# Graph attention kernel, first stage: transposing raw rows, normalisation moved behind the product with W, table written in half groups

## What is computed

```python
def _L0_gnn_ref(h, adj, W, a):
    Wh = h @ W
    a1, a2 = (a[:Fout, 0], a[Fout:, 0])
    e = (Wh @ a1)[:, None] + (Wh @ a2)[None, :]
    e = jnp.where(e > 0, e, ALPHA * e)
    e = jnp.where(adj > 0, e, MASK_VAL)
    attention = jax.nn.softmax(e, axis=1)
    return jax.nn.elu(attention @ Wh)

x = x + _L0_gnn_ref(_layernorm(x, axis=-1), adj, L0_gnn_W, L0_gnn_a)
x = x + _L0_ffn_ref((_layernorm(x, axis=-1))[None], ...)[0]
```

## Time and profile before

| | |
|---|---|
| median of three runs | 1185.75 us |
| profiled execution, span from first to last instruction | 1177.2 us |
| median less span (what lies around the instructions, and the spread between runs) | 8.55 us |
| first stage, up to the last table row (0 to 143.7 us) | 12% of the span |
| wait for the table to land | 143.7 to 160.2 us |
| second stage | about 160 to 1020 us |
| busy: PE, VectorE, ScalarE, GpSimd | 884.0, 891.8, 796.2, 655.2 us |
| DMA traffic | 357.33 MB, mean 304 GB/s |

### The profile page before, as it was taken

How to read it: one execution, slowest core, us unless ns; L and a number is a source line. 1 busy time by engine, 2 the same in 40 slices (tenths; PEclk the granted TensorE clock), 3 DMA queues, 4 the chain that set the end, 5 groups by cost and what they waited for, 6 DMA issues and landing times.

```text
span 1177.2 us, 24953 instructions
## 1 busy us (share of the span) xinstructions
PE 884.0 (75%) x4321; PEld 558.7 (47%) x4389; DVE 891.8 (76%) x4327; ACT 796.2 (68%) x1339; POOL 655.2 (56%) x700
## 2 busy tenths in 40 slices
PE   2777728788888878888788878876878765568995
PEld 1545514454444444544444444543544444346674
DVE  5788637888888888888788888876887876555563
ACT  1544639788878888888678887866887821146663
POOL 3555445565556556655566656654655656236664
PEclk9999959999999999999899999988998986679998
DMA  7678679999999999999899999988998995035551
GB/s 258 249 277 316 250 278 370 359 379 382 366 375 377 366 372 378 380 359 379 328 354 377 381 375 374 384 314 306 383 373 316 329 249 130 25 112 162 174 167 59
DMA packets 84715, 357.33 MB, mean 304 GB/s; under 512 B 26006, under 2 KB 52591, under 8 KB 68289
## 3 DMA queue, kind: packets, MB, share of 16 engines
q1 hardware_dynamic: 56226, 296.78, 67.9%
q0 software_dynamic: 27712, 60.06, 14.9%
q10 hardware_dynamic: 736, 0.05, 0.0%
HBM read 343.67 MB, written 32.05 MB: 319 GB/s over the span
## 4 chain that ended last, share of the span: by engine, by line
DVE 27%; DMA 22%; issue 21%; PE 9%; POOL 6%; DVEq 2%; POOLq 0%; ACT 0%; ACTq 0%
DMA regions<-x,posu 13%; DMA G_all<-wh_table,idx 7%; POOL G_all L617 4%; DVE top_word L900 2%; PE psO L1718 2%; DMA out_x<-raw_all,tok 2%; DVE xn L1170 2%; PE psO L1591 2%; POOL out_x L679 1%; DVE begun L1070 1%; DVE lidx L1185 1%; DVE oh L1193 1%; DMA wh_table<-mean_sb 1%; DVE el L1144 1%; DVE lmax L1180 1%
## 5 line engine op out<-in xcount | busy, mean ns | idle before, releaser
L617 POOL DMA_INDIRECT G_all<-wh_table,idx x384 | 397.7, 1036 | 137.8 <-issue 131.0
L725 ACT ACTIVATE sg<-raw_all,minus_tiny 128x1024 fp8e4<-128x1024 int32 x256 | 311.5, 1217 | 0.1
L728 ACT ACTIVATE sg<-raw_all,minus_half 128x1024 fp8e4<-128x1024 int32 x256 | 311.4, 1216 | 0.0
L1516 PE MATMUL psO<-word_no,share 128*128 128x512 bf16 x827 | 220.5, 397 | 3.7 <-issue 0.9
L639 POOL DMA_INDIRECT regions<-x,posu x64 | 67.4, 1053 | 209.2 <-DVE idx L1062 111.8
L1591 PE MATMUL psO<-G_all,diag 128*128 128x256 f32 x640 | 162.9, 404 | 22.3 <-DVE diag L1127 22.3
L1591 PEld LDWEIGHTS psO<-G_all,diag 128*128 128x128 f32 x640 | 123.6, 201 | 64.5 <-issue 48.3
L1525 PE MATMUL psF<-sg,fold_w 128*128 128x512 bf16 x512 | 136.5, 390 | 7.5 <-DVE top_word L900 2.7
L1516 PEld LDWEIGHTS psO<-word_no,share 128*128 128x128 bf16 x885 | 90.7, 107 | 86.4 <-issue 15.4
L758 ACT ACTIVATE pr<-ee,nmx 128x16 f32<-128x16 f32 x64 | 19.7, 308 | 153.9 <-DVE nmx L1118 153.9
L900 DVE MAX8 top_word<-psF 128x8 f32<-128x256 f32 x256 | 103.0, 425 | 15.4 <-remote 9.6
(11 more groups left out here) (227 smaller groups left out, 1901.7 us busy)
## 6 DMA issues: line engine op xcount, KB each, us to landing
raw_all<-in_adj SPq DMA_DIRECT2D x128, 2048.0 KB
raw_all<-regions SPq DMA_DIRECT2D x84, 130.0 KB, 2.1
wh_table<-G_all POOLq DMA_DIRECT2D x8, 1040.0 KB, 11.8
x_sb<-in_x SPq DMA_DIRECT2D x8, 1024.0 KB, 5.8
G_all<-wh_table,idx POOLq DMA_INDIRECT x384
regions<-pad_row SPq DMA_DIRECT2D x32, 130.0 KB
x_sb<-in_L_ffn_W SPq DMA_DIRECT2D x4, 512.0 KB
x_sb<-in_L_ffn_W SPq DMA_DIRECT2D x8, 256.0 KB
```

The source lines that it names most:

```text
L617: pool.indirect_dma_start(out=G[par][:, k, :], out_offset=None, in_=table[:, :], in_offset=bass.IndirectOffsetOnAxis(ap=idx[par][:, k:k + ...
L725: act.activation(sign_of[par][q][0], raw_of[b][q % 2][0], ACT.Identity, bias=minus_tiny[:, 0:1], scale=TINY, saturate=False)
L728: act.activation(sign_of[par][q][1], raw_of[b][q % 2][1], ACT.Sign, bias=minus_half[:, 0:1], saturate=False).then_inc(a_sg, 1)
L1516: pe.matmul(psO[par][:, :], share[:, :], word_no[:, 0:2, :].rearrange("p q w -> p (q w)"), start=True, stop=True)
```

## The change

- TensorE transposes the raw rows of `x_sb`; `normalise`, its four `xn` buffers and the semaphore `v_xn` are gone. The first product is then x·W' with W' = W_aug - (1/256)·(ones·W_aug), which equals (x - mean)·W_aug.
- W' is made once: TensorE multiplies a matrix of ones with `w_aug` (new line 1476), VectorE subtracts the result over 256 (new line 1025, two instructions on 128 x 258).
- The division by the deviation moves into the eviction: VectorE `table_rows` (new line 975) multiplies PSUM by `rs` where it copied. It stands first in each strip and has no lag; `COPY_LAG` is gone.
- Table rows go out in half groups (`CHUNK` = 4, 520 KB), right behind the fourth and the eighth strip, 16 issues for 8. `row_sum` adds up table rows (258 columns) for the first 60 strips; the last four are added by TensorE at the end, straight from `table_rows_sb`, so the mean row needs one product less.
- `load_group` waits only until the load before the last has landed (none for the first two).
- Set-up: TensorE waits for W and a alone and for five constants; the router matrix and bias have semaphores of their own. The clearing of `G_all` is cut to its two padding columns. `fold_w`, `word_no`, `rw_t`, `hT` and `count` move behind the statistics of group 0. Two small writes of a padding row into the table are gone.

```diff
-            sp.dma_start(w_raw[:, :, :], gW.rearrange("(h p) n -> p h n", p=P)).then_inc(const_in, 16)
+            sp.dma_start(w_raw[:, :, :], gW.rearrange("(h p) n -> p h n", p=P)).then_inc(w_in, 16)
 
             def load_group(g, par, i):
 
-                sp.wait_ge(v_xn, g * GROUP + 2)
-                sp.nop(nofuse=True)
+                if i:
+                    sp.wait_ge(xg_in[par], i * 16)
+                    sp.nop(nofuse=True)
                 sp.dma_start(x_sb[:, bass.ds(g * GROUP, GROUP), :],
                              x[bass.ds(g * GROUP * P, GROUP * P), :].rearrange("(r p) d -> p r d", p=P)
...
-            def row_sum(s, r):
-
-                pool.wait_ge(v_xn, s + 1 + 2 * GROUP)
+            def row_sum(g, par, r):
+
+                s = g * GROUP + r
+                pool.wait_ge(v_wh, s + 1 + 2)
                 if s:
                     pool.wait_ge(pl_sum, s)
                 pool.nop(nofuse=True)
-                pool.tensor_tensor(xn_sum[:, :], xn_sum[:, :], xn[r % 4][:, :], ALU.add).then_inc(pl_sum, 1)
-
-            def write_rows(g, par):
-
-                pool.wait_ge(v_wh, g * GROUP + GROUP + 2)
+                pool.tensor_tensor(row_total[:, :], row_total[:, :], table_rows_sb[par][:, r, 0:D + 2], ALU.add).then_inc(pl_sum, 1)
+
+            def write_rows(g, par, r):
+
+                pool.wait_ge(v_wh, g * GROUP + r + CHUNK + 2)
                 pool.nop(nofuse=True)
-                pool.dma_start(table[bass.ds(g * GROUP * P, GROUP * P), :].rearrange("(r p) d -> p r d", p=P),
-                               table_rows_sb[par][:, :, :]).then_inc(tab_out[par], 16)
+                pool.dma_start(table[bass.ds((g * GROUP + r) * P, CHUNK * P), :].rearrange("(r p) d -> p r d", p=P),
+                               table_rows_sb[par][:, r:r + CHUNK, :]).then_inc(tab_out[par], 16)
 
             def group(g, par, i, behind, ahead):
                 for r in range(GROUP):
-                    row_sum(g * GROUP + r, r)
-                    if behind and r == COPY_LAG - 1:
-                        write_rows(g - 1, 1 - par)
+                    if g * GROUP + r < NS - CHUNK:
+                        row_sum(g, par, r)
+                    if r % CHUNK == CHUNK - 1:
+                        write_rows(g, par, r - CHUNK + 1)
                     if ahead and r == 5:
                         inverse_stds(g + 1)
             groups(pool, group)
...
-                act.dma_start(a_sb[:, :, 0:1], ga[D:2 * D, :].rearrange("(h p) o -> p h o", p=P)).then_inc(const_in, 16)
-                act.dma_start(a_sb[:, :, 1:2], ga[0:D, :].rearrange("(h p) o -> p h o", p=P)).then_inc(const_in, 16)
-            act.dma_start(rw_sb[:, :], rw[:, :]).then_inc(const_in, 16)
-            act.dma_start(rb_sb[:, :], rb.rearrange("(o n) -> o n", o=1).to_broadcast([P, E])).then_inc(const_in, 16)
+                act.dma_start(a_sb[:, :, 0:1], ga[D:2 * D, :].rearrange("(h p) o -> p h o", p=P)).then_inc(w_in, 16)
+                act.dma_start(a_sb[:, :, 1:2], ga[0:D, :].rearrange("(h p) o -> p h o", p=P)).then_inc(w_in, 16)
+            act.dma_start(rw_sb[:, :], rw[:, :]).then_inc(rw_in, 16)
+            act.dma_start(rb_sb[:, :], rb.rearrange("(o n) -> o n", o=1).to_broadcast([P, E])).then_inc(rb_in, 16)
...
-            v.memset(xn_sum[:, :], 0.0)
+            v.memset(row_total[:, :], 0.0)
+            v.memset(G_all[:, :, D + 2:ROW], 0.0)
...
-            v.memset(G_all[:, :, :], 0.0)
-            v.wait_ge(consts, 19)
...
-            def normalise(g, par, r):
+            def table_rows(g, par, i, r):
                 s = g * GROUP + r
 
+                v.wait_ge(pe_wh, s + 1 + 2)
                 if r == 0:
                     v.wait_ge(pl_rs, g + 1)
-                if s >= 4:
-                    v.wait_ge(pe_xT, s - 1)
-                    v.wait_ge(pl_sum, s - 3)
-                v.tensor_scalar(xn[s % 4][:, :], x_rows(s), mv[par][:, r, 0:1], rs[par][:, r:r + 1],
-                                ALU.subtract, ALU.mult).then_inc(v_xn, 1)
-
-            def table_rows(s):
-                g, r = divmod(s, GROUP)
-                i, par = divmod(g, 2)
-
-                v.wait_ge(pe_wh, s + 1 + 2)
-                if r == 0:
-                    v.wait_ge(tab_out[par], i * 16 + 16)
-                v.tensor_copy(table_rows_sb[par][:, r, 0:D + 2], psW[r % 2][:, 0:D + 2]).then_inc(v_wh, 1)
+                    if i:
+                        v.wait_ge(tab_out[par], i * 16 * GROUP // CHUNK)
+                        v.wait_ge(pl_sum, g * GROUP - GROUP)
+                v.tensor_scalar(table_rows_sb[par][:, r, 0:D + 2], psW[r % 2][:, 0:D + 2], rs[par][:, r:r + 1], None,
+                                ALU.mult).then_inc(v_wh, 1)
...
-                    normalise(g, par, r)
+                    table_rows(g, par, i, r)
...
-                    if g * GROUP + r >= COPY_LAG:
-                        table_rows(g * GROUP + r - COPY_LAG)
...
+            for h in range(DH):
+                v.wait_ge(pe_w, DH + 1)
+                v.tensor_copy(w_aug[:, h, D:D + 2], psL[:, 2 * h:2 * h + 2]).then_inc(v_w, 1)
+
+            for h in range(DH):
+                v.wait_ge(pe_w, DH + 2)
+                v.scalar_tensor_tensor(out=w_aug[:, h, :], in0=psW[1][:, 0:D + 2], scalar=-1.0 / D, in1=w_aug[:, h, :],
+                                       op0=ALU.mult, op1=ALU.add).then_inc(v_w, 1)
+            v.wait_ge(consts, 19)
...
+
+            v.wait_ge(pe_w, DH + 4)
+            v.tensor_scalar(mean_sb[:, 0:D + 1], psL[0:1, 0:D + 1], 1.0 / N, None, ALU.mult).then_inc(v_wh, 1)
...
-            pe.wait_ge(const_in, 16 * 5)
-            pe.wait_ge(consts, 19)
+            pe.wait_ge(w_in, 16 * 3)
+            pe.wait_ge(consts, 5)
...
+            pe.wait_ge(v_w, 3 * DH)
+            pe.nop(nofuse=True)
             for h in range(DH):
-                mm = pe.transpose(psW[0][:, h * E:(h + 1) * E], rw_sb[:, h * P:(h + 1) * P], ident[0:E, 0:E])
+                mm = pe.matmul(psW[1][:, 0:D + 2], ones_f[:, :], w_aug[:, h, :], start=(h == 0), stop=(h == DH - 1))
...
+            def transposes(s, g, par, i, r):
+
+                if r == 0:
+                    pe.wait_ge(xg_in[par], i * 16 + 16)
                 if s >= 3:
                     pe.wait_ge(a_xT, s)
                 pe.nop(nofuse=True)
                 for h in range(DH):
-                    mm = pe.transpose(psXn[s % 3][:, h * P:(h + 1) * P], xn[s % 4][:, h * P:(h + 1) * P], ident[:, :])
+                    mm = pe.transpose(psXn[s % 3][:, h * P:(h + 1) * P], x_sb[:, s, h * P:(h + 1) * P], ident[:, :])
                 mm.then_inc(pe_xT, 1)
 
...
                 for r in range(GROUP):
-                    transposes(g * GROUP + r, r)
+                    transposes(g * GROUP + r, g, par, i, r)
+                    if g * GROUP + r == 2:
+                        pe.wait_ge(v_w, 4 * DH)
                     if g * GROUP + r >= 2:
                         table_rows(g * GROUP + r - 2, r)
+                if g == 0:
+                    pe.wait_ge(v_fold_w, 2)
                 fold(i, i % 2, par)
...
-            pe.wait_ge(pl_sum, NS)
+            pe.wait_ge(pl_sum, NS - CHUNK)
+            pe.wait_ge(v_w, 4 * DH + 1)
             pe.nop(nofuse=True)
-            for h in range(DH):
...
+            pe.matmul(psL[0:1, 0:D + 2], ones_f[:, 0:1], row_total[:, :], start=True, stop=False)
+            for r in range(GROUP - CHUNK, GROUP):
+                pe.wait_ge(v_wh, NS - GROUP + r + 1 + 2)
+                pe.nop(nofuse=True)
+                mm = pe.matmul(psL[0:1, 0:D + 2], ones_f[:, 0:1], table_rows_sb[(NG - 1) % 2][:, r, 0:D + 2], start=False,
+                               stop=(r == GROUP - 1))
             mm.then_inc(pe_w, 1)
```

79 lines of the change are left out of this document (28 added, 51 removed).

## The result

The changed kernel takes 1154.57 us (median of 4 executions, 1146.12 to 1163.13) beside 1185.24 for the kernel before (4, 1184.41 to 1191.76): ratio 0.971, 95% interval 0.965 to 0.978, so 30.7 us faster. Forecast: 1152, range 1142 to 1168. The profiled execution took 1156.93 us with a span of 1155.2. Medians are of all executions; a ratio and its interval leave out executions more than 1.5% above the quickest of their kernel, so the two can differ by some tenths of a per cent.

What follows compares the result with a forecast made beforehand. The first stage was held bound by a ring of waits, the second near the DMA limit. A gather 35 us earlier, less 1 for emptier buffers, took the span from 1177.2 to 1143; plus 8.55 made 1152 us, range 1142 to 1168.

Steps and rivals of the forecast that it cites:

- Set-up: Start of the kernel: first eviction at about 18.8 us against 29.3, 10.5 us earlier, bounds 7 and 13.
- Group 0: First eight strips: four at 2.1 us, four at 1.1, a fold of 1.2; end at about 31 instead of 42.5.
- Odd groups: Groups 1, 3, 5 and 7 of the first stage: 10.3 us each, TensorE's pace in the last group.
- loads and clock: End of the first stage: 2 us added to 108, putting the last table row at 110 us.
- Even groups: Groups 2, 4 and 6, where VectorE also decodes: 12 us each, with no charge for table-write waits.
- the port rule: VectorE and GpSimd share a port pair locked per instruction; 0.6 us per group was to go with normalise.
- rival 1: First stage becomes DMA-bound: groups of 13 us, gather near 133, gain 27 or less, about 1160 us; chance 0.14.
- End of the stage: Last table row at 110 us, mean row issued 1.7 later and landing in 11, first gather at 125 instead of 160.2.
- Ring: First stage: waits among normalise, TensorE's transposes and products, and VectorE's evictions bind it, not DMA or a peak engine.
- GpSimd's power exposed in each group: First stage: GpSimd's chain binds in seven groups, costing 19 us of the 34, about 1170 us; chance 0.07.
- Writes one after another: First stage: half table writes land serially at 11.8 us each, 57 us later than 160, about 1240 us; chance 0.03.
- Second stage gives it back by the clock: Second stage: denser TensorE work lowers the granted clock earlier, costing 18 us, about 1170 us; chance 0.06.

Runs made afterwards that it cites:

- again: The changed kernel run once more, nothing altered, on the first chip: 1152.54 us, ratio 0.973 to the kernel before.
- again2: The changed kernel run once more, nothing altered, in the third group on a slower chip: 1241.33 us, ratio 0.976 to the kernel before.
- late37: The changed kernel with GpSimd additions that nothing needs ahead of the first gather: 1180.79 us, ratio 0.999 to the kernel before.
- setup_back: The changed kernel with the old set-up: all of G_all cleared, TensorE waiting for every small load: 1160.4 us, ratio 0.980 to the kernel before.
- gate: The changed kernel with each load of x held until the second eviction two groups earlier; slower chip: 1246.59 us, ratio 0.976 to the kernel before.
- dummy: The changed kernel with the removed normalise put back on VectorE, its output unread; slower chip: 1253.63 us, ratio 0.983 to the kernel before.
- before_free: The kernel before with one edit, loads of x waiting only for the load before the last: 1184.16 us, ratio 1.007 to the kernel before.

## Why the prediction was right

- **Set-up: right.** TensorE at 6.90 (forecast 6.8), first eviction at 19.64 (18.8), at 20.5 to 20.7 in `again` and `again2`. The product with ones took 2.06 us (2), the corrections 0.76 (0.9). Undone, the set-up costs 6.9 us at the first eviction and 6.8 at the gather, less than the 10.5 that I gave it: even so the first eviction is at 27.54, not at 29.27, so 1.7 us of its gain are not the set-up's.
- **Group 0: end at 29.2 for 31.** "I take four strips at 2.1 us" was too much. It depends on when TensorE comes to its upper level. Here is the first strip's product in the first profile:

```profile
18.49 1.11 PE L1501 MATMUL psW<-w_aug,xT 128*128 128x258 f32 x4 [1.09 <-issue]
```

and in `again2`:

```profile
18.43 2.06 PE L1501 MATMUL psW<-w_aug,xT 128*128 128x258 f32 x4 [1.09 <-issue]
```

In `again2` the first strip took the 2.1 us, the second 1.40, and the others run as in the first profile, so group 0 ended at 30.3. The view prints a clock of 1.00 for both from 0 on, but line 1476 took 2.06 us there too: for the start the durations tell more than that column. The "768 ns" of the forecast is the longest record, not the level: where the view shows 0.50 (121.8 to 124.3 us of the kernel before), line 1507's records took 636 to 639 ns for 382 at 1.00.
- **Odd groups: right.** 9.8 and 10.1 us for 10.3; TensorE is the bound, 10.10 of 10.10 us busy. Group 7 took 11.3 in the first profile, with TensorE busy throughout at a granted clock of 0.85, and 9.6 in `again` and `again2`; this was the 1 to 2 us for "loads and clock".
- **Even groups: the term that was too small.** I took 12; they took 14.5, 13.1 and 12.6, together 4.2 us more than the forecast, and the seven groups 81.5 for 77. Two things were missing. The first is the wait for a table write, for which I had said "no charge": 3.0 us in group 2 and 1.0 in group 4. In `again2` no group has one, and the even groups took 13.1, 12.6 and 12.6. What remains there, 2.3 us, has the size of the second: I had used the port rule for `normalise` and then written "the sum above holds this already". It held a part. The decoding is stretched too, by 1.0 to 1.7 us per group. In the trace of the kernel before two of its instructions show this, and I hadn't asked for them (VectorE, 42 to 144 us; line 966, the copy, took 686 ns for 174):

```profile
L941 DVE SCALAR_TENSOR_TENSOR key<-bits,code 128x128 f32<-128x128 int32 x3 | 2.5, 825 | 0.1
```

These 1.0 us were in the group length from which I subtracted; the change added the stretch of lines 902 and 914 in groups 4 and 6. That length was read from stretches that are not the groups, as said above: 16.1 us less 3.87 is 12.2, so my 12 came out nearly as it would have. "Group 5 at 16 us" behind the upper bound and rival 1 took 14.0.
- **End of the stage: two errors of opposite sign.** Last table row at 110.7 (110). The mean row was issued 2.8 us after it (1.7) and landed in 8.62 (11; 8.5 to 10.7 in `again`, `again2`, `late37`, `setup_back` and `gate`); first gather at 123.1 for 125.
- **What bounded it: right.** Ring, not busy time alone (`dummy`) and not loads (`before_free`, `gate`). DMA was near: a share of 0.93 in the stage and 1.03 in groups 3 and 4, at 384 to 404 GB/s. The 358 GB/s of the Trainium skill, "DMA: Bandwidth & Descriptors", "Where 436 GB/s comes from", would have put the gather near 129 (an estimate), and the measured rates are above it.
- **Rivals.** DMA-bound: no, group 3 took 10.1 us at a share of 1.03. GpSimd's power exposed in each group: no, 2.1 us in the whole stage. Writes one after another: no, 9.0 us in the median and 3.9 us of waits. Second stage gives it back by the clock: 4 to 10 us are given back by medians, but on the second chip the clock is the same in both. By my own sign, a second stage more than 5 us longer than 1017, this part of the forecast failed in the first profile (1032.1), where the granted clock was 0.92 for 0.93; in the second (1015.4) it didn't.
- **Where the 1152 came from.** 37.1 us were gained at the gather where I had 35, and about 6 lost behind it where I had 1: 31 for 34. That the total came out within 3 us is partly luck, since these errors offset each other and the four executions spread over 17 us. The last step also carried a slip: "plus the 8.55 between span and median". Only 1.7 us lie around a span; the rest was that the profiled execution of before (about 1178.9 us, its span and these 1.7) was quicker than the median. It went into both kernels' times alike and did no harm.
